# Cross-attention and FFN on one core: the order of values, V halves, output tiles and FFN products within even and odd slots

## The reference, cut to what matters

```
h = layernorm(x)
q = h @ Wq; k = ctx @ Wk; v = ctx @ Wv          # 512 -> 4096, 1024, 1024
q, k = rope(q), rope(k)                          # cos/sin rows gathered by position
p = softmax(where(mask == 0, -1e9, q @ k.T / sqrt(128)))
x = x + (p @ v) @ Wo                             # 4096 -> 512
h = layernorm(x)
r = softmax(h @ gate_w.T)                        # 8 experts
x = x + ((h * (r @ in_scale)) @ sign(W).T) * (r @ out_scale) + bias
```

## Time and profile before

| | |
|---|---|
| median of 3 runs | 1145.2 us (1145.05 to 1145.42) |
| the profiled execution | 1146.23 us |
| its span, first to last instruction | 1144.3 us |
| busy: TensorE, its weight loads | 99%, 83% |
| busy: VectorE, ScalarE, GpSimd | 71%, 47%, 62% |
| DMA | 105 MB, 92 GB/s |

### The profile page before, as it was taken

The page is one execution under the profiler, slowest core; times in us unless marked ns, Lnnn a source line. Parts: engine busy times, 40 slices in busy tenths (PEclk is TensorE's granted clock), DMA queues, the critical chain, the costliest instruction groups (busy, mean ns, idle before and its releaser), DMA issues.

```text
span 1144.3 us, 22925 instructions
## 1 busy us (share of the span) xinstructions
PE 1132.6 (99%) x7935; PEld 955.1 (83%) x7935; DVE 813.3 (71%) x1366; ACT 537.0 (47%) x1736; POOL 704.8 (62%) x585
## 2 busy tenths in 40 slices
PE   9999999999999999999999999999999999999998
PEld 8778888888888888888888888888888888888877
DVE  5876876767687766877767676677767767776577
ACT  4554454454544454444553535544444544445443
POOL 5855675555667556675665666566675556755544
PEclk9999999999999999999999999999999999999999
DMA  8323332333323223333422323333232222322301
GB/s 243 103 85 101 115 122 79 90 97 92 91 82 102 75 82 84 123 107 93 116 81 73 103 74 86 98 99 114 84 89 78 75 83 75 86 80 74 93 20 38
DMA packets 134483, 105.29 MB, mean 92 GB/s; under 512 B 10680, under 2 KB 109256, under 8 KB 134400
## 3 DMA queue, kind: packets, MB, share of 16 engines
q1 hardware_dynamic: 128848, 93.72, 28.4%
q10 hardware_dynamic: 4784, 8.40, 2.2%
q0 software_dynamic: 768, 2.10, 0.6%
HBM read 100.00 MB, written 4.19 MB: 91 GB/s over the span
## 4 chain that ended last, share of the span: by engine, by line
PE 93%; DVE 3%; issue 2%; ACT 1%; POOL 1%; DMA 1%; ACTq 0%; DVEq 0%; POOLq 0%
PE chunk L1256 22%; PE chunk L1258 21%; PE chunk L1257 21%; PE duo_ps L1332 6%; PE duo_ps L1245 3%; PE o_ps L1355 3%; PE aux L1245 2%; PE duo_ps L1355 2%; PE chunk L1308 1%; PE chunk L1310 1%; PE chunk L1309 1%; DVE swp L943 1%; PE o_ps L1310 1%; PE o_ps L1309 1%; PE o_ps L1308 1%
## 5 line engine op out<-in xcount | busy, mean ns | idle before, releaser
L455 POOL TENSOR_TENSOR w_lo<-raw,w_hi 128x512 fp32r<-128x512 f32 x192 | 247.7, 1303 | 314.7 <-ACT w_hi L598 312.3
L943 DVE TENSOR_TENSOR swp<-chunk,sinT 64x512 f32<-64x512 f32 x320 | 220.3, 688 | 51.2 <-PE chunk L1258 32.1
L598 ACT ACTIVATE w_hi<-raw 128x512 fp32r<-128x512 f32 x192 | 116.6, 630 | 274.3 <-PE chunk L1258 208.8
L1256 PE MATMUL chunk<-xT_hi,w_hi 128*128 128x512 f32 x512 | 206.7, 404 | 1.5 <-POOL w_lo L455 1.5
L1258 PE MATMUL chunk<-xT_hi,w_lo 128*128 128x512 f32 x512 | 200.3, 391 | 0.0
L1257 PE MATMUL chunk<-xT_lo,w_hi 128*128 128x512 f32 x512 | 199.7, 390 | 0.0
L1256 PE MATMUL chunk<-wo_hi,oT_hi 128*128 128x512 f32 x492 | 195.1, 396 | 1.2 <-DVE oT_lo L877 1.2
L1258 PE MATMUL chunk<-wo_hi,oT_lo 128*128 128x512 f32 x492 | 191.9, 390 | 0.0
L1257 PE MATMUL chunk<-wo_lo,oT_hi 128*128 128x512 f32 x492 | 191.7, 390 | 0.0
L635 ACT ACTIVATE probs<-scores,neg_max 128x64 f32<-128x64 f32 x512 | 170.4, 337 | 41.1 <-DVE neg_max L899 41.1
L462 POOL TENSOR_TENSOR qT<-qT,swp 128x512 f32<-128x512 f32 x127 | 163.8, 1297 | 34.6 <-DVE qT L945 34.0
(11 more groups left out here) (284 smaller groups left out, 2046.5 us busy)
## 6 DMA issues: line engine op xcount, KB each, us to landing
raw<-in_L_xattn_Wq SPq DMA_DIRECT2D x128, 256.0 KB, 2.8
raw<-in_L_xattn_Wo SPq DMA_DIRECT2D x128, 256.0 KB, 2.7
raw<-in_L_xattn_Wk SPq DMA_DIRECT2D x32, 256.0 KB, 2.8
raw<-in_L_xattn_Wv SPq DMA_DIRECT2D x32, 256.0 KB, 3.0
acc<-in_x ACTq DMA_DIRECT2D x14, 256.0 KB, 2.7
x_tile<-in_x SPq DMA_DIRECT2D x12, 256.0 KB, 2.9
c_tile<-in_ctx SPq DMA_DIRECT2D x12, 256.0 KB, 3.2
result<-y ACTq DMA_DIRECT2D x12, 256.0 KB, 2.0
```

Of the source, the lines that this page charges most:

```text
L455: nc.gpsimd.tensor_tensor(lo, raw[:, r, :], hi.bitcast(F32), ALU.subtract).then_inc(wsplit_lo, 1)
L598: return nc.scalar.activation(dst, src, ACT.Copy)
L943: last = nc.vector.tensor_tensor(swp[to, k, :], bank[of, :], sinT[to, here], ALU.mult)
L1256: nc.tensor.matmul(bank, a_hi, b_hi, start=opens and i == 0, stop=False)
```

## The change

Even slots: on TensorE the queries 2, 3 and 4 now come one after the other (with the route transpose between 3 and 4), then values, in-scales, the first V half, out-scales, the second V half, and last the FFN product. V's halves go to `chunk[0]` and `chunk[1]` and wait for the rotations of queries 2 and 3. VectorE rotates all queries before it splits the outcome of values, and splits V at the end of the even slot. ScalarE and GpSimd are reordered to fit.

Odd slots: TensorE starts with the scores; all four output tiles come behind the scores and the side job's transposes, and output tiles 0 and 1 wait for the V splits. Without `s.ffn`, the side jobs' calls fall away and the order is otherwise the same.

```diff
@@ -135,7 +135,7 @@
         sc_ps, tr_ps = (duo_both[:, i, :] for i in range(2))
 
         DUO_BANK, TABLE_BANK = [sc_ps, tr_ps], o_ps[1]
-        V_BANK, FIRST_V_BANK = [chunk[1], o_ps[0]], [chunk[0], sc_ps]
+        V_BANK, FIRST_V_BANK = [chunk[0], chunk[1]], [chunk[0], sc_ps]
         OUTPUTS = [o_both, duo_both]
         C_BANK, X_BANK = [aux, sc_ps, tr_ps, o_ps[0]], [sc_ps, tr_ps, aux, chunk[2]]
         X_ORDER = [0, 2, 1, 3]
@@ -522,23 +522,26 @@
                     rope_sum(s, 0)
                     split_lo(s, 6 if s.odd else 5)
                     rope_sum(s, 1)
-                    if not s.odd:
-                        split_lo(s, 6)
+                if s.proj and s.odd:
                     split_lo(s, 7)
-                if s.ffn:
-                    xs_lo_split(f[0], in_slot)
-                if s.proj:
+                    if s.ffn:
+                        xs_lo_split(f[0], in_slot)
                     split_lo(s, 8)
                     rope_sum(s, 2)
-                if s.proj and s.odd:
                     rope_sum(s, 3)
                     if s.number != SLOTS - 1:
                         rope_sum(s, 4)
                 if s.proj and not s.odd:
+                    split_lo(s, 6)
+                    rope_sum(s, 2)
+                    split_lo(s, 7)
+                    rope_sum(s, 3)
+                    split_lo(s, 8)
+                    rope_sum(s, 4)
                     split_lo(s, 9)
+                    if s.ffn:
+                        xs_lo_split(f[0], in_slot)
                     split_lo(s, 10)
-                    rope_sum(s, 3)
-                    rope_sum(s, 4)
                 if s.ffn:
                     add_residual(*f, in_slot)
                 if s.number == 1:
@@ -775,28 +778,32 @@
                 if not s.odd:
                     split_hi(s, 5)
                 split_hi(s, 6)
-                out_hi(s, 0)
-                out_hi(s, 1)
-                if s.ffn:
-                    route_hi(f[0], in_slot)
                 if s.odd:
+                    out_hi(s, 0)
+                    out_hi(s, 1)
+                    if s.ffn:
+                        route_hi(f[0], in_slot)
                     split_hi(s, 7)
-                out_hi(s, 2)
-                out_hi(s, 3)
-                if s.odd:
+                    out_hi(s, 2)
+                    out_hi(s, 3)
                     split_hi(s, 8)
+                    if s.ffn:
+                        xs_split(f[0], in_slot)
+                        out_scales(f[0], in_slot)
                 else:
                     split_hi(s, 7)
-                if s.ffn:
-                    xs_split(f[0], in_slot)
-                if not s.odd:
+                    if s.ffn:
+                        route_hi(f[0], in_slot)
                     split_hi(s, 8)
+                    for p in range(PAIRS):
+                        out_hi(s, p)
                     split_hi(s, 9)
                     split_hi(s, 10)
-                if s.ffn:
-                    out_scales(f[0], in_slot)
-                if not s.odd:
+                    if s.ffn:
+                        xs_split(f[0], in_slot)
                     v_hi_split(s, 0)
+                    if s.ffn:
+                        out_scales(f[0], in_slot)
                     v_hi_split(s, 1)
                 if s.ffn:
                     store(f[0], in_slot)
@@ -1059,10 +1066,6 @@
                     for j in range(1, KQ):
                         rotate(s, j)
                     return scales_lo()
-                if s.odd:
-                    even = Slot(s.q, s.g - 1, False, False, odd=0)
-                    v_lo_split(even, 0)
-                    v_lo_split(even, 1)
                 if s.intake:
                     pick_positions(t[0])
                     x_stats(t[0])
@@ -1070,8 +1073,8 @@
                     dve.wait_ge(added, s.q * KVH * PAIRS)
                     f_stats(*f, in_slot)
                     f_norm(*f, in_slot)
-                add_out(s, 0)
                 if not s.odd:
+                    add_out(s, 0)
                     add_out(s, 1)
                 soft_a(s, 0)
                 soft_a(s, 1)
@@ -1079,12 +1082,17 @@
                     c_lo_split(*t)
                     x_norm(t[0])
                 if s.odd:
+                    add_out(s, 0)
+                    soft_b(s, 0)
                     add_out(s, 1)
-                soft_b(s, 0)
-                add_out(s, 2)
-                add_out(s, 3)
-                soft_b(s, 1)
-                if not s.odd:
+                    add_out(s, 2)
+                    soft_b(s, 1)
+                    add_out(s, 3)
+                else:
+                    soft_b(s, 0)
+                    add_out(s, 2)
+                    add_out(s, 3)
+                    soft_b(s, 1)
                     rotate(s, 0)
                 pT_lo_split(s, 0)
                 if s.ffn and s.odd:
@@ -1110,22 +1118,24 @@
                     rotate(s, 4)
                 else:
                     rotate(s, 1)
-                    if s.ffn:
-                        route_lo(f[0], in_slot)
                     if s.intake:
                         x_lo_split(*t)
                     rotate(s, 2)
+                    rotate(s, 3)
+                    if s.ffn:
+                        route_lo(f[0], in_slot)
+                    rotate(s, 4)
                     out_lo(s, 0)
+                    out_lo(s, 1)
                     if s.ffn:
                         scale_in(f[0], in_slot)
-                    rotate(s, 3)
-                    out_lo(s, 1)
                 out_lo(s, 2)
                 out_lo(s, 3)
                 if s.number == SLOTS - 1:
                     last_rope_sum(s, KQ - 1)
                 if not s.odd:
-                    rotate(s, 4)
+                    v_lo_split(s, 0)
+                    v_lo_split(s, 1)
                 if s.ffn:
                     finish(f[0], in_slot)
                 if isinstance(s.g, int) and s.g == 1 and s.proj and s.number != 1:
@@ -1271,10 +1281,10 @@
                     pe.wait_ge(added, n - 2)
                 elif s.after_last:
                     pe.wait_ge(added, (s.U - 3) * PAIRS + p + 1)
+                elif p < 2 and s.odd:
+                    pe.wait_ge(v_ok, s.U + p)
                 elif p == 0:
                     pe.wait_ge(cos_done, (s.U - 1) * KQ + 3)
-                elif p == 1 and s.odd:
-                    pe.wait_ge(v_ok, s.U)
                 elif p == 1:
                     pe.wait_ge(cos_done, (s.U - 1) * KQ + 4)
                 else:
@@ -1294,11 +1304,11 @@
                 if i == 0:
                     pe.wait_ge(wsplit_lo, split_count(s, max(loads_of(s).index(c) for c in (V_OWN, V_NEXT))))
                     if not s.first_proj:
-                        pe.wait_ge(cos_done, s.U * KQ + 4)
+                        pe.wait_ge(cos_done, s.U * KQ + 3)
                 elif s.first_proj:
                     pe.wait_ge(x_lo, 1)
                 else:
-                    pe.wait_ge(o_lo, (s.U - 1) * PAIRS + 2)
+                    pe.wait_ge(cos_done, s.U * KQ + 4)
                 lowest = min(entry(s, V_OWN), entry(s, V_NEXT))
                 both = slice(lowest, WRING, 1 if s.first_proj else 2)
                 for t in range(2):
@@ -1478,8 +1488,8 @@
                 if s.first_attn:
                     return first_attention(s)
                 t, f = (job and job[0] for job in jobs_of(s)[:2])
-                out_proj(s, 0)
                 if not s.odd:
+                    out_proj(s, 0)
                     out_proj(s, 1)
                 scores_of(s, 0)
                 scores_of(s, 1)
@@ -1503,25 +1514,37 @@
                     t_x(t)
                 if s.ffn:
                     t_logits(f, in_slot)
-                project(s, 1 if s.odd else 2)
-                values(s, 0)
-                values(s, 1)
-                if s.ffn:
-                    t_route(f, in_slot)
-                project(s, 2 if s.odd else 3)
-                if s.ffn:
-                    t_in_scales(f, in_slot)
-                project(s, 3 if s.odd else 4)
-                if s.ffn:
-                    t_out_scales(f, in_slot)
                 if s.odd:
+                    project(s, 1)
+                    values(s, 0)
+                    values(s, 1)
+                    if s.ffn:
+                        t_route(f, in_slot)
+                    project(s, 2)
+                    if s.ffn:
+                        t_in_scales(f, in_slot)
+                    project(s, 3)
+                    if s.ffn:
+                        t_out_scales(f, in_slot)
                     project(s, 4)
+                    if s.ffn:
+                        t_product(f, in_slot)
                 else:
+                    project(s, 2)
+                    project(s, 3)
+                    if s.ffn:
+                        t_route(f, in_slot)
+                    project(s, 4)
+                    values(s, 0)
```

(10 more changed lines are left out.)

## The result

The changed kernel takes 1150.55 us (median of 5 runs, 1150.4 to 1151.6), the kernel before 1145.16 (1145.05 to 1145.42): a ratio of 1.0048, 95% interval 1.0036 to 1.0059. That is 5.4 us more; 7.4 were forecast.

The account below looks back on a forecast made before the run. TensorE, busy 1132.6 of 1144.3 us, was taken as the bound. 8.4 - 0.9 - 0.1 = +7.4 us on the 1145.2 us median gave 1152.6 us; likeliest case 1150.2 to 1155, with the first two rivals 1150.2 to 1158.5.

Parts of the forecast that it names:

- The stall of the FFN transposes: Six odd FFN slots: transposes wait for VectorE's normalized tile, 1.4 us each, 8.4 us in all.
- S: Start of the scores in a changed odd FFN slot; finish forecast at S + 0.11, transposes at S + 3.40.
- The norm at 0.55 us, not 1.49: VectorE's norm in changed odd FFN slots was taken at the shorter of two lengths seen before.
- The first rival: Norm collides with GpSimd's weight split in changed odd slots: stall 2.34 us, +13.0 us, 1158.2 us; chance 0.10.
- Even FFN slots, -0.15 us each: Net of the removed V-half wait and the added route step in six even FFN slots, -0.9 us in all.
- The 0.24 at the V half: Wait of the first V half's weight load on a query rotation, 0.24 us in six even FFN slots, removed.
- Route's step: Last matmul ahead of route's transpose between queries 3 and 4 takes 0.32 us instead of 0.23: +0.09 each.
- From V half to output tile: The step from V half to output tile, 0.24 us against 0.23, goes 15 times: -0.1 us.
- V's neighbours: V halves standing behind values or in-scales in 15 even slots: bounded at 1.4 us either way, taken as 0.
- Other waits of the even slots: All put at nothing; tightest was out-scales waiting for scale_in, with 0.5 us left over.
- The second rival: New wait, scale_in before out-scales or xs_lo before the product, 0.5 us in six slots: +10.4, 1155.6 us; chance 0.08.
- the third rival: Not slower: savings in TensorE's switching costs around values and V pay for the stall; chance 0.05.

Follow-up runs that it names:

- e3: Changed kernel with the odd tile's FFN statistics moved into the even slot between the V splits, and GpSimd's root ahead of the residual sum: 1142.32 us.
- e4: Changed kernel with output tile 0 back ahead of the FFN transposes in odd FFN slots, on TensorE: 1143.19 us.
- e1: Changed kernel with GpSimd's root of the next FFN tile ahead of the even tile's residual sum, statistics left in place: 1156.23 us.
- e9: Kernel before the change with only the even slots' FFN product moved behind the second V half: 1146.40 us.
- e6: Kernel before the change with the odd slots' change alone, scores first and all output tiles later, even slots as before: 1176.42 us.
- e5: Changed kernel with the odd slots' start undone, output tile 0 ahead of the scores again, even slots still changed: 1142.79 us.
- e7: e3 with values moved between queries 3 and 4, ahead of the route transpose, in even FFN slots: 1148.37 us.
- e10: Changed kernel with the FFN product put back between the two V halves: 1176.36 us.

## Why the prediction was right, and where its sizes were off

- **The stall of the FFN transposes, 8.4 us: right.** 3.40 us from scores to transposes in place of 2.02, six times 1.38, is 8.3. Finish at S + 0.11 and transposes at S + 3.40 are what was forecast; the norm ends at S + 3.35. e3 and e4 take the stall away in two ways (the chain shorter, the cover longer) and both end under the kernel before; that it is the cause is shown.
- **The norm at 0.55 us, not 1.49: right**, and e1 shows what it turns on. The first rival's 13.0 us did not come, since in the changed order the norm starts after the residual sum, and in all six odd slots the next weight split starts 0.9 us or more after the norm does. The rival's mechanism is real: e1 meets it with the sum, e9 and e6 with the split.
- **Even FFN slots, -0.15 us each: the mis-sized term.** The pair with FFN, stall apart, gave 0.38 us (1.00 - 1.38), six times 2.3 us in place of 0.9. The 0.24 at the V half went as forecast. Route's step was booked with the wrong sign: it gave 0.06 instead of costing 0.09, since the last step of the projection ahead is not lengthened (631.28 to 631.52, 0.23 us). The rest are small neighbours: three projections -0.12, the output tiles of the odd slot -0.12, in-scales +0.11 (they now stand behind values, where route stood), product +0.09, V halves -0.04.
- **Why route's price was misread.** The prediction took the 0.32 us step from places ahead of scores and values, and booked it as the price of plain fp32. The kernel before had the counterexample. The transposes of the probabilities, plain fp32 like route's, also come right behind a projection, and there the step is 0.23:

```profile
623.68 0.40 PE L1258 MATMUL chunk<-xT_hi,w_lo 128*128 128x512 f32 x1
623.91 1.03 PE L1245 MATMUL duo_ps<-ident,probs 128*128 128x128 f32 x8
```

  The long step stands only where matmuls of 128*64 (scores) or 64*128 (values) come next, and values are fp32r and have it all the same. So in these traces it goes with the shape and not with the format; no run varies the shape alone.
- **From V half to output tile, -0.1 us over 15 pairs: too small.** I counted only the step of 0.24 against 0.23. Output tile 0 stood between V and the scores, with the long last step of 0.32; gone from there it takes 2.72 us instead of 2.84. Most of that comes back, since V now stands behind values (2.97 for that half where a projection behind values took 2.85) and the scores behind V (its last step 0.21 instead of 0.12). Eight pairs without FFN are 0.06 to 0.12 shorter and the last 0.02, together 0.7 us. e5 keeps the old odd slots and has 66.86 us a pair, against 66.80 in e3: the odd part of it is 0.06.
- **Together:** 8.3 - 2.3 - 0.7 = +5.3 us, against 8.4 - 0.9 - 0.1 = +7.4. The bound given for V's neighbours was 1.4 us either way, and of the error of 2.1 us route's step is 0.9 and its neighbours and V's are the rest; the time fell inside the range, near its low end.
- **Other waits of the even slots, nothing: right, with little to spare.** Out-scales started at 639.50, `scale_in` ended 637.90 + 0.68 = 638.58: 0.92 us left, where 0.5 was reckoned. e7 takes 1.6 away and gets the wait. The second rival is excluded for this kernel, and its mechanism shown.
- **Not slower (the third rival): its mechanism exists, its size was missing.** The even slots and V's neighbours gave 3.0 us, with route's step and the six waits in them, where 6 were needed. Without the stall it would have held: e3 and e5 are faster than the kernel before.
- **One reason given for the stall was incomplete.** I named two edits, the output tile moved and the product moved. e9 shows that the product's place alone brings only 1.1 us of stall, as the output tile still covers it. But e10 shows that putting it back does not help either: with V's splits in the even slot, finish is behind V's end wherever the product stands. The place of finish in VectorE's order ties the chain to the slot's end just as firmly as the product's.
- **Two small slips of the prediction.** The V splits before were done 1.5 us into the odd slot (645.99 against 644.47), not 1.6, and V's neighbours at -1.4 with a chain 0.15 shorter give 1150.3 as the low end, not 1150.2. Neither changes anything else.

## What to carry to other kernels

When work is moved away from ahead of a consumer, take the producer's whole chain from the trace and count it from its first releaser, through each in-order queue it passes; here the output tile moved away (2.84 us) against 0.06 to spare would have been a stall of 2.8. It became 1.4, because the chain, free of the V splits and with its norm at 0.55 us, now ends 3.35 us into the slot and not 4.80. Then look which links of the chain need the releaser at all: statistics and root never needed the product, and only when both stood ahead of it (one on each engine) did 8 us come back. Half of such a fix can be worse than none (e1). And when a step's price is read off one place, look for a second place with the same cause before it goes into a sum.

## What the runs showed of the hardware

- **The clock fell behind some stalls of 2.5 us and behind none of 2.0.** Idle times of 1.3 us (the changed kernel) and 2.0 us (e1) left the granted clock at 1.00, as did the 1.6 us of the earlier trace rows. Idle times of 2.5 to 2.7 us were followed by 0.50 in two of six slots in e6 and in five of six in e10, 0.1 to 1.5 us after the matmuls had begun again. It lasted 3.4 us each time, at 0.43 us a matmul of 512 columns in place of 0.23. That adds about 1.6 us to the stall, more than half of its length again. Why one slot of e10 and four of e6 were spared is open: within a run their idle times are the same to 0.05 us. In e10 TensorE also idles 1.5 us for the product, some 7 us ahead of the stall, and in e6 it doesn't; no run separates that.
- **Of VectorE's norm and GpSimd's work, the first to start keeps its time.** The twelve runs traced hold 144 such norms (line 991 and its copies). The 55 that started 0.02 to 0.07 us behind a GpSimd instruction of 512 columns took 1.48 to 1.53 us and ended 0.28 to 0.29 us after it. The 89 that met none at their start took 0.54 to 0.55. When the norm is first, the sum pays only 0.14 (e3).
- **In the slots the last step ahead of scores or values is 0.09 us longer, whatever stands there.** It is 0.32 instead of 0.23 for a projection, an output tile or the product, and 0.21 instead of 0.12 for a V half. From a projection to route, in-scales, out-scales or the transposes of probabilities, all 128*128, it is 0.23 to 0.24.
- **A single plain fp32 transpose costs little on the step ahead of it:** route between two projections takes 0.03 us itself, and the step before it is 0.23. The step behind it is 0.32 (631.54 to 631.86), as behind a group of transposes.
